# Four softmax block copies moved to VectorE, with value sums, casts and products in another order, in a two-layer attention and feed-forward kernel

## What is computed

```python
x = _rmsnorm(hidden_states, ln_weight)
h_q = (x @ w_q.T).reshape(b, lq, H, DH)
h_k = (key_value_states @ w_k.T).reshape(b, lk, H, DH)
h_v = (key_value_states @ w_v.T).reshape(b, lk, H, DH)
score = jnp.einsum('bqhd,bkhd->bhqk', h_q, h_k) + position_bias[None]
score = jnp.where(m, score, -jnp.inf)
score = jnp.where(m, jax.nn.softmax(score, axis=-1), 0.0)
attn = jnp.einsum('bhqk,bkhd->bqhd', score, h_v).reshape(b, lq, H * DH)
out = attn @ w_out.T
return hidden_states + out
```

## Time and profile before

| | |
|---|---|
| median of 3 runs | 944.47 us (944.09 to 944.98) |
| the profiled execution | 945.47 us, its span 943.6 us |
| TensorE, weight loads | 915.7 us (97%), 789.4 (84%) |
| VectorE, ScalarE, GpSimd | 676.5 (72%), 662.5 (70%), 512.0 (54%) |

### The profile page before, as it was taken

How to read it: one execution, slowest core, us unless ns; L and a number is a source line. 1 busy time by engine, 2 the same in 40 slices (tenths; PEclk the granted TensorE clock), 3 DMA queues, 4 the chain that set the end, 5 groups by cost and what they waited for, 6 DMA issues and landing times.

```text
span 943.6 us, 17334 instructions
## 1 busy us (share of the span) xinstructions
PE 915.7 (97%) x5277; PEld 789.4 (84%) x5277; DVE 676.5 (72%) x1221; ACT 662.5 (70%) x2043; POOL 512.0 (54%) x582
## 2 busy tenths in 40 slices
PE   8899999979999999999999999999999998999997
PEld 7778888868888888888888888888889887878885
DVE  5658576556787677777866787678767877777787
ACT  5788775757777777777777778776867776335664
POOL 3352535438465846485557555756576553133477
PEclk9999999999999999999999999999999999999999
DMA  9215236853767466755676467647764765130101
GB/s 333 86 68 184 70 110 240 313 175 131 264 227 243 171 223 221 249 208 190 232 239 215 170 244 237 223 154 256 246 226 156 266 208 179 69 123 1 35 23 68
DMA packets 61292, 171.71 MB, mean 182 GB/s; under 512 B 6055, under 2 KB 8491, under 8 KB 60988
## 3 DMA queue, kind: packets, MB, share of 16 engines
q1 hardware_dynamic: 61244, 171.11, 52.1%
HBM read 159.56 MB, written 11.53 MB: 181 GB/s over the span
## 4 chain that ended last, share of the span: by engine, by line
PE 76%; DVE 11%; ACT 6%; issue 4%; POOL 1%; DMA 1%; DVEq 0%; SPq 0%; ACTq 0%; POOLq 0%
PE ps_s L2227 6%; PE ps_o L2206 6%; PE ps_o L2207 5%; PE ps_o L2211 5%; PE ps_q L372 5%; PE ps_v L372 5%; PE ps_q L374 5%; PE ps_q L373 5%; PE ps_v L374 5%; PE ps_v L373 5%; PE ps_k L372 5%; PE ps_k L373 4%; PE ps_k L374 4%; PE ps_t L2255 4%; ACT scores L796 3%
## 5 line engine op out<-in xcount | busy, mean ns | idle before, releaser
L814 ACT COPY probs_t<-scores 32x128 f32<-32x128 f32 x720 | 213.4, 296 | 33.1 <-DVE scores L1635 24.5
L796 ACT ACTIVATE scores<-scores,neg_max 128x128 f32<-128x128 f32 x256 | 99.8, 391 | 116.5 <-DVE neg_max L1623 116.4
L1619 DVE TENSOR_TENSOR scores<-ps_s,shift 128x512 f32<-128x512 f32 x64 | 44.3, 692 | 115.6 <-PE ps_s L2227 115.6
L1180 POOL TENSOR_TENSOR wq_lo<-raw_q,wq_hi 128x256 fp32r<-128x256 f32 x65 | 48.0, 739 | 127.2 <-ACT wq_hi L629 127.2
L2206 PE MATMUL ps_o<-wo_hi,att_hi 128*128 128x512 f32 x256 | 102.7, 401 | 7.7 <-DVE acc L1510 5.6
L1510 DVE TENSOR_TENSOR acc<-ps_o,acc 128x512 f32<-128x512 f32 x128 | 87.1, 681 | 28.6 <-PE ps_o L2211 28.6
L2207 PE MATMUL ps_o<-wo_lo,att_hi 128*128 128x512 f32 x256 | 100.4, 392 | 0.0
L1139 POOL TENSOR_TENSOR shift<-bias_sb,mask_sb 128x512 f32<-128x512 f32 x64 | 84.5, 1322 | 1.4 <-DVE scores L1619 1.4
L372 PE MATMUL ps_v<-wv_hi,ct_hi 128*128 128x256 f32 x264 | 77.3, 293 | 6.6 <-DVE v_odd_low L1583 2.4
L803 ACT ACTIVATE scores<-scores,row_fac 128x128 f32<-128x128 f32 x240 | 76.9, 393 | 4.6 <-DVE row_fac L1629 4.5
L2211 PE MATMUL ps_o<-wo_hi,att_lo 128*128 128x512 f32 x256 | 79.2, 391 | 0.0
(11 more groups left out here) (398 smaller groups left out, 2835.1 us busy)
## 6 DMA issues: line engine op xcount, KB each, us to landing
ring_hi<-scratch_x_t SPq DMA_DIRECT2D x39, 512.0 KB, 4.5
ring_lo<-scratch_x_t SPq DMA_DIRECT2D x39, 512.0 KB, 5.4
ring_hi<-scratch_c_t SPq DMA_DIRECT2D x39, 512.0 KB, 5.4
ring_lo<-scratch_c_t SPq DMA_DIRECT2D x39, 512.0 KB, 6.2
raw_o<-in_w_o SPq DMA_DIRECT2D x16, 512.0 KB, 3.3
raw_q<-in_w_q SPq DMA_DIRECT2D x15, 512.0 KB, 3.6
raw_k<-in_w_k SPq DMA_DIRECT2D x15, 512.0 KB, 4.9
xt_hi<-scratch_x_t SPq DMA_DIRECT2D x13, 512.0 KB, 6.7
```

The source lines that it names most:

```text
L796: e = act.activation(probs[n][:, m, :], scores[n][:, m, :], ACT.Exp, bias=neg_max[:, n, m:m + 1], accum_out=row_sum[:, n, m:m + 1])
L814: last = act.copy(block_of(probs_t, j, i), block_of(scores[n], i, j))
```

## The change

ScalarE now copies only the eight blocks whose row and column lie in different halves of the matrix; VectorE copies the four others, (1,0), (0,1), (3,2) and (2,3), right behind its two transposes, and TensorE's `step_values` waits for both. Beside that:

- ScalarE: `split_qk` in steps 0 to 7 ahead of `pt_blocks`; `high_v1` of the second turn behind `scale_rows` and `high_fourth`; the scaling of step 60 is made by ScalarE and not by VectorE.
- VectorE: the value copy `v_evac(2, 1, 0)` ahead of the transposes; in the turns `v_c12`, `v_c21(i, 1)`, `q_c21` behind the add of the first output half, `k_u3` earlier; in the second turn the value copies 12 and 13 in other places.
- TensorE: the second output half of step 0 behind the scores of step 2; the k product `k_p4` between two output halves in the second turn and in the last.

```diff
-            return 4 * s + n if turned(s) else 4 * WHOLE + 3 * (s - WHOLE) + n
+            return 5 * s + n if turned(s) else 5 * WHOLE + 3 * (s - WHOLE) + n
...
-                        if j != i:
+                        if j != i and i // 2 != j // 2:
                             last = act.copy(block_of(probs_t, j, i), block_of(scores[n], i, j))
...
+                if s % 4 < 2:
+                    split_qk(g + 1, s % 4)
                 pt_blocks(s, s % 2)
...
-                if c == 3 and coming:
+                if c == 3 and coming and own:
                     high_v1(i + 1)
...
+                if c == 3 and not own:
+                    high_v1(i + 1)
...
             attention_high(STEPS - 5)
+            scale_rows(STEPS - 4, 0, p_done)
...
                 dve.transpose(flat(probs[n]), flat(probs[n])).then_inc(p_done, 1)
+                dve.wait_ge(p_done, s + 1)
+                for i in range(4):
+                    last = dve.tensor_copy(block_of(probs_t, i ^ 1, i), block_of(scores[n], i, i ^ 1))
+                last.then_inc(s_chain, 1)
...
+                if s == 0:
+                    v_evac(2, 1, 0)
                 if s > 0:
                     attention_rest(s - 1)
                 turn_blocks(s, n)
-                if s == 0:
-                    v_evac(2, 1, 0)
...
-                if c == 4 and not last:
-                    if own:
-                        v_c21(i, 1)
-                    else:
-                        v_evac(13, 2, 1, done=16)
...
-                    if c == 3:
-                        v_evac(12, 2, 0, done=15)
+                if c == 7:
+                    k_u3(G)
...
+                if not turned(s):
+                    row_factors(s, n)
                 attention_rest(s - 1)
-                if c == 3:
-                    q_c21(G)
...
                     turn_blocks(s, n)
-                else:
-                    softmax_back(s, n)
...
                 add_output(s - 1, (c - 1) % LOOP_STEPS, (0,))
+                if c == 1 and own:
+                    v_c12(i, 0)
+                if c == 2:
+                    if own:
+                        v_c12(i, 1)
+                    else:
+                        v_evac(12, 2, 0, done=15)
+                if c == 3:
+                    q_c21(G)
                 if c % 4 == 3:
                     k_c21(G)
+                if c == 3 and not last:
+                    if own:
+                        v_c21(i, 1)
...
                 pe.wait_ge(pt_out, s + 1)
+                if turned(s):
+                    pe.wait_ge(s_chain, chain(s, 5))
...
-            output(0, 0, 0)
+            output(0, 0, 0, (0,))
...
+                if s == 2:
+                    output(0, 0, None, (1,))
...
-                    k_p4(G)
+                    if own and not last:
+                        k_p4(G, 1)
...
+                if c == 3:
+                    if own and not last:
+                        v_p4(i, 1)
+                    else:
+                        k_p4(G, 1)
```

More of the change, by code:

```diff
@@ L798, in exponentials, with scale_rows @@
                 e.then_inc(e_done, 1)
-            def scale_rows(s, n):
+            def scale_rows(s, n, signal=scaled):
                 act.wait_ge(s_chain, chain(s, 3))
@@ L803, in scale_rows @@
                     e = act.activation(probs[n][:, m, :], probs[n][:, m, :], ACT.Identity, scale=row_fac[:, n, m:m + 1])
-                e.then_inc(scaled, 1)
+                e.then_inc(signal, 1)
             def pt_blocks(s, n):
@@ L848, in step_first @@
                     split_o(1)
-                if s % 4 < 2:
-                    split_qk(g + 1, s % 4)
                 if s % 4 == 1:
@@ L1658, in step_first @@
                 turn_blocks(s, n)
-                if s == 0:
-                    v_evac(2, 1, 0)
-                else:
+                if s > 0:
                     add_output(s - 1, (s - 1) % LOOP_STEPS, (0,))
@@ L1773, in step @@
                     turn_blocks(s, n)
-                else:
-                    softmax_back(s, n)
[L1776 to L1782, removed]
+                if c == 1 and not own:
+                    v_evac(14, 3, 0, done=13)
                 if c == 5 and coming:
@@ L1785, in step @@
                 add_output(s - 1, (c - 1) % LOOP_STEPS, (0,))
-                if c == 7:
-                    k_u3(G)
+                if c == 1 and own:
[7 more added lines that the diff above has]
+                    q_c21(G)
                 if c % 4 == 3:
                     k_c21(G)
+                if c == 3 and not last:
+                    if own:
+                        v_c21(i, 1)
+                    else:
+                        v_evac(13, 2, 1, done=16)
                 if c % 4 == 2:
@@ L2330, in q_p4, with k_p4 @@
                 unit_q(ps_q, 0, ring_hi[1], ring_lo[1])
-            def k_p4(G):
+            def k_p4(G, sums):
                 pe.wait_ge(wk_lo_s, 7 * G - 10)
                 pe.wait_ge(ring_in[2], 64 * G - 112)
-                pe.wait_ge(k_comb, 7 * G - 19)
+                pe.wait_ge(k_comb, 7 * G - 20 + sums)
                 unit_k(ps_k, 0, part(xt_hi, 0, HALF), part(xt_lo, 0, HALF))
@@ L2536, in step @@
                     k_p2(G)
-                if c == 3 and own and not last:
-                    v_p4(i, 1)
+                if c == 3:
+                    if own and not last:
+                        v_p4(i, 1)
+                    else:
+                        k_p4(G, 1)
                 if c == 4 and coming:
@@ L2546, in step @@
                 if c == 7:
-                    k_p4(G)
+                    k_p4(G, 2)
                 output(s - 1, (c - 1) % LOOP_STEPS, None, (1,))
```

## The result

The changed kernel takes 1025.6 us (median of 4 runs, 1023.22 to 1026.48) against 944.28 us (944.09 to 944.98) for the kernel before: ratio 1.0856 [1.0836, 1.0875], slower. The forecast was 1022 us. The profiled execution took 1023.22 us with a span of 1021.4, 77.8 more than before.

What follows compares the result with a forecast made beforehand. TensorE's own work, busy 97% of the span, was taken as the bound. 945.5 us less 11 for moves plus 89 for copies over 6.5 turns is 1023.5, less 1.0 to the median: 1022; 8 in 10 between 936 and 1050.

Steps and rivals of the forecast that it cites:

- The price of a copy: VectorE in the loop: 0.2 us with GpSimd idle; otherwise each of four copies lets one queued GpSimd instruction pass; chance 0.62.
- one wait: VectorE's four copies wait once together, or not at all: 938.5 us, between 932 and 944; chance 0.25.
- the one in between: Two GpSimd instructions pass instead of four, gaps of some 0.85 us a step: about 973 us, 944 to 985; chance 0.13.
- the 3 that I named as a sign: Sign of being right: the four copies take some 3 us of VectorE a step in the loop.
- The working of step 2: Step 2 of the turn at 351 us, copies and GpSimd alternating: add ends at 388.95, gap grows by 2.5 us.
- The eight gaps: TensorE's gaps before the second output half, counted for each step of a loop turn: growth of 14.6 us a turn.
- the high end of the range: Upper end of 985 to 1055 us: adds granted-clock drops in the loop, some 1.5 us each, up to three a turn.
- The sign that I set: Sign of being right: TensorE waits for acc in most steps, 80 us or more in total.
- The head: Steps 0 to 7: GpSimd mostly idle behind the transposes, a value product ahead of the second half; nothing counted for copies.
- The moves: Reordered work in head, second turn and tail takes 11 us off; in the loop 0.6 and 0.2 us a turn.
- Term (a): Head: casts of the next q and k weights ahead of probability copies end two waits for wk_lo, 2.9 us.
- (f): Loop: last value sum at the end of a step's VectorE work saves about 0.6 us a turn, and 0.2 before scores.

Runs made afterwards that it cites:

- the reduction: The changed kernel with VectorE's four block copies each made by a maximum over an axis of one element, same place: 954.57 us, ratio 1.0106.
- moves alone: The changed kernel without VectorE's four copies, all twelve block copies on ScalarE again and all other moves kept: 923.17 us, ratio 0.9773.
- the sums put back: The changed kernel with all twelve copies on ScalarE and value sums of loop steps 1, 3 and 4 where the kernel before has them: 932.59 us.

## Why the prediction was right

*The bound.* Right. TensorE's products are untouched, and the time follows the gaps.

*The price of a copy.* Right in both parts. I took 0.2 us with GpSimd idle; the median is 0.22. The estimate by the Trainium skill's page "VectorE: DVE Perf Modes", errata section, 0.13 us, was too low; the section itself says beneath its table that this row under-predicts. I took one GpSimd instruction per copy, as long as one is queued; step 2 shows it copy by copy, and the reduction shows that this waiting is the larger part of the loss. Two of the three cases, one wait and the one in between, are thereby out. The copies take 2.4 us a step in the loop, not the 3 that I named as a sign.

*The working of step 2.* The order was right, its length too long. I had 4.7 us from the end of the transposes to the end of the add, and it is 3.9 (410.22 to 414.12). I added copy and GpSimd instruction, 0.95 us a round; they overlap, and a round takes 0.70. The gap grew by 1.9 us, not 2.5. With the second half wanted 2.24 us behind the transposes in both kernels, the room was read rightly.

*The eight gaps.* Steps of the loop's second turn, after less moves alone, in us:

| step | 0 | 1 | 2 | 3 | 4 | 5 | 6 | 7 | sum |
|---|---|---|---|---|---|---|---|---|---|
| counted | 1.1 | 1.7 | 2.5 | 1.6 | 0.95 | 1.9 | 2.5 | 2.3 | 14.6 |
| measured | 0.97 | 1.70 | 1.87 | 1.87 | 0.42 | 3.67 | 1.83 | 2.22 | 14.6 |

The sum is right by errors that cancel. Steps 2, 4 and 6 were counted 0.5 to 0.7 too long, which three rounds of 0.70 for 0.95 us would explain; step 1, where all four copies are held up too, came out as counted all the same, and why was not looked into. Step 5 is 1.8 longer than counted: 1.53 of it is the drop of the clock, which I had only in the high end of the range, though at the price it has (1.5). Its gap has another cause than the one that I named: VectorE owes TensorE a value sum ahead of the add, and that comes 1.88 us late. Without the drop the turn would have grown by 13.0, not 14.6: that the sum is the counted one to a tenth is luck. The sign that I set, 80 us or more of waits for acc, failed as it stands: 61.0, and 72 with the value sum's; much of the rest of the cost is not a listed wait.

*The head.* Wrong. I counted nothing for the copies in steps 0 to 7 because GpSimd would be idle; it cost 7.5 us, in steps 1, 2, 3 and 5 (2.8, 1.7, 0.8 and 2.3). GpSimd's instructions there are up to 2.38 us long and do stand behind the transposes: at 111.04 four copies took 5.82 us, each ending 0.08 to 0.09 us behind a GpSimd instruction (of 2.38, 1.29, 1.29 and 1.26 us). Step 1 has a drop of the clock as well, and the waits for att_hi are 3.3 us longer in the head than in the moves alone.

*The moves.* The direction was right, the size too small: 16.2 us by my terms (11, and 0.8 in each of 6.5 turns), 22.3 measured. Head, second turn and tail gave 4.0, 6.3 and 1.0, in all 11.2 for the 11. Term (a) was wrong inside that sum: I had both waits for wk_lo end, 2.9 us, but 2.4 us in two places remain in the moves alone and 1.6 in the changed kernel, which is also a sign of mine that failed; the other terms gave that much more. The step that was mis-sized is (f): 2.0 us a turn, not 0.8. In the kernel with the sums put back, the starts of TensorE's matmuls show three gaps a turn: 0.63, 0.40 and 0.85 us from start to start where 0.23, 0.12 and 0.23 are usual, each followed by 0.34 for 0.23. That is 1.6 of the 1.7 us that came back. The table of waits shows only the part behind the end of the matmul before, 3.5 us in five turns (2.3 for the value sum, 1.2 for acc), and of these I had counted the value sum's alone.

*The sum.* Too little taken off (16.2 for 22.3) and too little put on (94.9 for 100.1, of which 7.5 lie in the head) cancel: 78 us counted between the profiled executions, 77.8 measured. The mechanism was right, the closeness is luck. The 3.6 us by which the median lies over 1022 are of another kind: the profiled execution of the changed kernel was the fastest of its four, 2.4 us below their median, and I had taken 1.5 us off for the one before.

*ScalarE.* Right in the loop, where its relief gains nothing; 1.2 us in the head.

Not settled: what makes a gap end in a drop. From the start of the last matmul to the start of the next, step 5 has 2.26 to 2.28 us in every turn of the loop; a drop follows in the first three turns and none in the last two. Step 7 has the longer 2.45 us in every turn, and a drop follows in the fourth alone:

```profile
700.73 0.72 PE L2213 MATMUL ps_o<-wo_hi,att_hi 128*128 128x512 f32 x1 [2.07 <-DVE acc L1513]
701.10:704.50 3.40, 3.40 (x13) 2.82 (x13) 0.18 (x1) 0.00 (x0) 3.32 (x4) 0.54 0.87 301
```

That drop costs 1.6 us, spread over step 7 (13.58 us instead of 12.42) and the step behind it (14.29 instead of 13.85).

## What to carry to other kernels

Before giving VectorE small SBUF copies, look at what GpSimd has queued at that moment: in this kernel 176 of 240 copies waited for a GpSimd instruction, and a row of four waited four times where GpSimd had enough queued, so their price was GpSimd's instruction (0.7 us) and not their own (0.2). Work taken from an engine that nobody waited for gained next to nothing here; put ahead of the one result that the bounding engine wants, it costs its full length once the room is used up, and even cheap work there was not free. When a change mixes moves and added work, time the moves by themselves: here 21 us of gain lay under a loss of 102.

## What was not expected of the hardware

- A maximum over an axis of one element moves a 32x128 block in 277 ns, all 240 times, and never waits for GpSimd, where the copy takes 220 ns or, on average, 595.
- Seven times in the changed kernel, behind gaps of TensorE of 2.3 to 3.6 us, the granted clock stood at 0.5 for 3.4 us. In the moves alone, with no gap of that length in the loop, it stays at 1.00 there. The gap of 2.3 us in step 5 with its drop makes the step 3.7 us longer.
- `neg_max` averages 515 ns in the changed kernel, 755 in the kernel before and 766 in the moves alone, which gives VectorE 15 us back. Most of that is not the new copies letting GpSimd pass: with VectorE's copies left out, and ScalarE's row of copies as short, it is 575. That it comes from ScalarE's casts, and so GpSimd's instructions, standing earlier behind the shorter row was not tested by itself.
